# A test-time-training layer with a gated expert layer on one core: order of the expert slots and of the ending

## The reference

```python
xn = layernorm(x)
s  = attn(xn)                    # 32 heads of 8 channels, a recurrence over 16 chunks of 16 tokens
g  = silu(moe(xn))               # 8 experts, top 2, hidden width 128
out = x + s * g

# attn, per head and chunk (state W1 8x8, b1 8):
Z1      = xk @ W1 + b1
grad    = ln_fused_l2_bwd(Z1, xv - xk, ln_w, ln_b)       # needs mean and deviation of Z1
Z1_bar  = xq @ W1 - eta * tril(xq @ xk.T) @ grad + b1 - tril(eta) @ grad
W1, b1  = W1 - (eta_last * xk).T @ grad, b1 - sum(eta_last * grad)
rows    = xq + ln(Z1_bar, ln_w, ln_b)
# attn, at the end: out = ln(rows, post_w, post_b) @ o_w.T
```

## Time and profile before

| | |
|---|---|
| time, median of 3 runs | 230.91 us (230.84 to 236.54) |
| profiled execution | 232.3 us, of which span from first to last instruction 230.4 us |
| busy in the span | PE 84%, DVE 86%, ACT 48%, POOL 67% |
| granted TensorE clock, mean | 0.937 of full speed |

### The profile page before, as it was taken

How to read it: one execution, slowest core, us unless ns; L and a number is a source line. 1 busy time by engine, 2 the same in 40 slices (tenths; PEclk the granted TensorE clock), 3 DMA queues, 4 the chain that set the end, 5 groups by cost and what they waited for, 6 DMA issues and landing times.

```text
span 230.4 us, 5314 instructions
## 1 busy us (share of the span) xinstructions
PE 194.5 (84%) x1893; PEld 154.6 (67%) x1893; DVE 198.2 (86%) x542; ACT 111.7 (48%) x219; POOL 154.3 (67%) x212
## 2 busy tenths in 40 slices
PE   8734999778489989599999998999798599998772
PEld 6513666256488869577977886889586488866551
DVE  2999999999993999999999999999999999306961
ACT  2461279642428263447534976355464456147220
POOL 2314539898659749495876289879999776464234
PEclk9965999999889999889988999999999799979998
DMA  5995200226622000365030043103000300400022
GB/s 177 372 405 170 69 4 0 49 56 139 209 42 81 3 0 9 93 109 76 9 92 3 0 100 138 48 6 92 4 4 6 93 3 0 149 36 3 0 92 91
DMA packets 26001, 17.45 MB, mean 76 GB/s; under 512 B 10552, under 2 KB 24312, under 8 KB 25464
## 3 DMA queue, kind: packets, MB, share of 16 engines
q1 hardware_dynamic: 25464, 16.25, 24.9%
q10 hardware_dynamic: 512, 0.87, 1.2%
HBM read 15.22 MB, written 1.87 MB: 74 GB/s over the span
## 4 chain that ended last, share of the span: by engine, by line
DVE 63%; PE 20%; issue 8%; ACT 3%; DMA 2%; POOL 2%; DVEq 0%; POOLq 0%; SPq 0%; ACTq 0%
DVE bank L833 7%; DVE pr L885 7%; DVE dW L890 7%; DVE pr L822 6%; PE bank L1179 6%; PE bank L1220 4%; PE bank L1138 3%; PE bank L1192 3%; DMA small<-in_small 2%; DVE QP L774 2%; DVE S L849 2%; PE bank L1206 2%; PE bank L1256 2%; DVE bank L880 2%; DVE bank L876 1%
## 5 line engine op out<-in xcount | busy, mean ns | idle before, releaser
L1179 PE MATMUL bank<-xn_hi,gup_hi 128*128 128x256 f32 x128 | 41.0, 321 | 2.4 <-ACT up L583 2.4
L1192 PE MATMUL bank<-down,hT 128*128 128x256 f32 x128 | 35.4, 403 | 4.1 <-ACT G L587 3.7
L351 POOL TENSOR_TENSOR gw<-gate,share 128x256 f32<-128x256 f32 x32 | 23.3, 728 | 22.1 <-ACT gate L582 21.4
L1179 PE MATMUL bank<-xn_lo,gup_hi 128*128 128x256 f32 x128 | 36.9, 289 | 0.0
L1179 PE MATMUL bank<-xn_hi,gup_lo 128*128 128x256 f32 x128 | 36.9, 288 | 0.0
L291 POOL TENSOR_TENSOR A<-A,mask 128x256 f32<-128x256 f32 x32 | 23.3, 734 | 10.7 <-ACT A L566 10.6
L1179 PEld LDWEIGHTS bank<-xn_hi,gup_hi 128*128 128x128 f32 x128 | 25.0, 196 | 8.0 <-issue 4.9
L1192 PEld LDWEIGHTS bank<-down,hT 128*128 128x128 f32 x128 | 23.5, 202 | 6.6 <-issue 3.8
L566 ACT ACTIVATE A<-bank,one 128x256 f32<-128x256 f32 x32 | 15.1, 471 | 25.2 <-PE bank L1138 25.2
L356 POOL TENSOR_TENSOR hT<-gw,up 128x256 f32<-128x256 f32 x32 | 23.4, 730 | 4.0 <-PE bank L1192 1.7
L1179 PEld LDWEIGHTS bank<-xn_hi,gup_lo 128*128 128x128 f32 x128 | 25.2, 197 | 0.3
(11 more groups left out here) (159 smaller groups left out, 429.8 us busy)
## 6 DMA issues: line engine op xcount, KB each, us to landing
wblk<-w_blocks SPq DMA_DIRECT2D x8, 512.0 KB, 3.9
share<-shares SPq DMA_DIRECT2D x8, 512.0 KB, 8.4
sgpad<-in_gup SPq DMA_DIRECT2D x1, 1024.0 KB, 9.5
G<-in_gup SPq DMA_DIRECT2D x1, 1024.0 KB, 11.6
down<-in_down SPq DMA_DIRECT2D x1, 1024.0 KB, 14.3
xkT<-in_x_bt SPq DMA_DIRECT2D x1, 1024.0 KB, 4.9
out<-G SPq DMA_DIRECT2D x4, 256.0 KB, 2.4
wkv<-in_wkv ACTq DMA_DIRECT2D x1, 512.0 KB, 4.0
```

Of the source, the lines that this page charges most:

```text
L351: pool.tensor_tensor(gw[:, :], gate[:, i % 2, :], share[:, pair % 2, e, :], ALU.mult).then_inc(S_["gw"], 1)
L1179: ins = pe.matmul(bank[4 + i % 2][:, 2 * P * g:2 * P * g + 2 * P], w[:, k, e, NI * g:NI * g + NI].bitcast(F32R), x[:, k, 2 * pair:2 * pair ...
L1192: ins = pe.matmul(bank[7][:, HS * r:HS * r + HS], hT[:, i % 2, P * r:P * r + P], down[:, e, :], start=(e == 0 and r == 0), stop=(e == NE - ...
```

## The change

1. **ScalarE, loop**: for j = 2, 3, 5 and 6 the slot behind tile 4 (slots 6, 11, 21 and 26) goes ahead of the square root table and `step_std(2j+2)`. In j = 4 the gate of slot 14 goes ahead of `half_out(0)`.
2. **TensorE, loop**: `group_end(j-1)` goes behind tile 2 and, for j > 1, behind the second slot of the group; for j = 1 it goes behind tile 2.
3. **GpSimd**: `pad_grads(7)` goes ahead of the last `hidden_product`.
4. **Ending**: ScalarE moves rows 2 and 3 (behind `norm_z(1)`, ahead of `output_rows(3)`), not VectorE; the sums of squares go by halves of the heads, the first of them behind the first square alone; both roots wait for both sums; all eight `gate_rows` stand behind the last `post_rows`; rows 0 and 1 are projected into bank 6; three more products of zeros stand between the last transposes and the last projections; the last row's addition is VectorE's; the last two rows are written by a DMA each.

```diff
@@ sync
-            for f in range(0, NF, 2):
+            for f in range(0, NF - 2, 2):
                 sp.wait_ge(S_["fin"], f + 2)
                 sp.dma_start(out_d[:, f:f + 2, :], G[:, f:f + 2, :]).then_inc(S_["out"], 16)
-            sp.wait_ge(S_["out"], 16 * NF // 2)
+            sp.wait_ge(S_["fin"], NF - 1)
+            sp.dma_start(out_d[:, NF - 2, :], G[:, NF - 2, :]).then_inc(S_["out"], 16)
+            sp.wait_ge(S_["fin_last"], 1)
+            sp.dma_start(out_d[:, NF - 1, :], G[:, NF - 1, :]).then_inc(S_["out"], 16)
@@ gpsimd
+                if j == NG - 1:
+                    pad_grads(NG - 1)
                 for i in slots:
                     hidden_product(i)
-            pad_grads(NG - 1)
             half_scale(1)
             pool.wait_ge(S_["xt"], 16)
-            for f in range(NF):
+            for f in range(NF - 1):
                 residual(f)
@@ scalar, norm_z, post_rows and loop
-                    act.wait_ge(S_["zv"], 2 * u + k + 1)
+                    act.wait_ge(S_["zv"], 2 * u + 2)
...
-                act.wait_ge(S_["yTp"], f + 1)
+                act.wait_ge(S_["yTp"], f + 1 if f >= 4 else 4)
...
                     scores_out(j, 2)
+                    expert_slot(slots.pop(0))
                     if j == 4:
                         half_out(0)
-                    expert_slot(slots.pop(0))
                 scores_out(j, 3)
                 expert_slot(slots.pop(0))
                 if j != 4:
                     scores_out(j, 4)
+                if slots and j != 4 and j < NG - 1:
+                    expert_slot(slots.pop(0))
                 if j < NG - 1:
                     preload_sqrt(2 * j + 1)
                     step_std(2 * j + 2)
...
             norm_z(1)
+            post_rows(2)
+            post_rows(3)
             output_rows(3)
@@ vector
+                sums = zv[:, :, :].rearrange("p w (k h) -> p (w k) h", k=2)
+                squares = zsq.rearrange("p w (k h d) -> p (w k) h d", k=2, d=HD)
                 for k in range(2):
-                    v.wait_ge(S_["zc"], 4 * u + 2)
-                    v.tensor_reduce(zv[:, k, :], zsq[:, k, :].rearrange("p (a d) -> p a d", d=HD), AX.X,
+                    v.wait_ge(S_["zc"], 4 * u + k + 1)
+                    v.tensor_reduce(sums[:, :, HH * k:HH * k + HH], squares[:, :, HH * k:HH * k + HH, :], AX.X,
                                     ALU.add).then_inc(S_["zv"], 1)
...
             half_variance(1)
-            post_rows(2)
-            post_rows(3)
             second_half_rows(0)
-            gate_rows(0, 2)
             second_half_rows(1)
             half_normalise(1, 0)
             half_normalise(1, 1)
-            gate_rows(2, 4)
             post_rows(6)
             post_rows(7)
-            gate_rows(4, NF)
+            gate_rows(0, NF)
+            v.wait_ge(S_["xt"], 16)
+            v.wait_ge(S_["res"], NF)
+            v.tensor_tensor(G[:, NF - 1, :], G[:, NF - 1, :], x_tok[:, NF - 1, :], ALU.add).then_inc(S_["fin_last"], 1)
@@ tensor
-                if f < B:
-                    pe.wait_ge(S_["yTv"], 8)
-                else:
-                    pe.wait_ge(S_["yTa"], 4)
-                    pe.wait_ge(S_["yTv"], 12)
+                pe.wait_ge(S_["yTv"], 4 * (f // B) + 4)
+                pe.wait_ge(S_["yTa"], 4 * (f // B) + 4)
...
                 tile(j, 1)
-                if j == 1:
-                    expert_slot(slots.pop(0))
-                group_end(j - 1)
                 if 2 <= j < NG - 2:
                     next_pair_rows(j + 2)
-                tile(j, 2)
                 if j > 1:
+                    tile(j, 2)
                     expert_slot(slots.pop(0))
+                else:
+                    expert_slot(slots.pop(0))
+                    tile(j, 2)
+                group_end(j - 1)
                 tile(j, 3)
...
             for f in range(4, NF):
                 post_channels(f)
+            zero_products(3, 2)
             for f in range(4, NF):
                 project(f)
```

More of the change, by code:

```diff
@@ L191, in build @@
             sgT sgp z0 z zc shareTp shareTc share_d share00 share01 share10 share11 gu gact gw h y g
-            zg zv zs zr orow post0 osum ov os yn yTp yTa yTv o res fin out"""
+            zg zv zs zr orow post0 osum ov os yn yTp yTa yTv o res fin fin_last out"""
         S_ = {n: sem("s_" + n) for n in names.split()}
@@ L205, in y_rows, with o_rows @@
             return bank[f_bank(f)][:, P * k:P * k + P]
+        def o_rows(f):
+            return bank[6][:, 256 * f:256 * f + 256] if f < 2 else bank[f_bank(f)][:, 256:512]
         @block.sync
@@ L277, in _ @@
                     sp.dma_start(x_tok[:, :, :], x_bt_d).then_inc(S_["xt"], 16)
-            for f in range(0, NF, 2):
+            for f in range(0, NF - 2, 2):
                 sp.wait_ge(S_["fin"], f + 2)
                 sp.dma_start(out_d[:, f:f + 2, :], G[:, f:f + 2, :]).then_inc(S_["out"], 16)
-            sp.wait_ge(S_["out"], 16 * NF // 2)
+            sp.wait_ge(S_["fin"], NF - 1)
+            sp.dma_start(out_d[:, NF - 2, :], G[:, NF - 2, :]).then_inc(S_["out"], 16)
+            sp.wait_ge(S_["fin_last"], 1)
+            sp.dma_start(out_d[:, NF - 1, :], G[:, NF - 1, :]).then_inc(S_["out"], 16)
+            sp.wait_ge(S_["out"], 16 * (NF // 2 + 1))
         @block.gpsimd
@@ L989, in gate_rows @@
                 for f in range(first, end):
-                    v.wait_ge(S_["o"], f + 1)
+                    v.wait_ge(S_["o"], max(f + 1, 2))
                     v.wait_ge(S_["g"], f // 2 + 1)
-                    v.tensor_tensor(G[:, f, :], bank[f_bank(f)][:, 256:512], G[:, f, :], ALU.mult).then_inc(S_["res"], 1)
+                    v.tensor_tensor(G[:, f, :], o_rows(f), G[:, f, :], ALU.mult).then_inc(S_["res"], 1)
             post_count = [0]
@@ L1249, in project @@
             def project(f):
-                if f < B:
-                    pe.wait_ge(S_["yTv"], 8)
-                else:
-                    pe.wait_ge(S_["yTa"], 4)
-                    pe.wait_ge(S_["yTv"], 12)
+                pe.wait_ge(S_["yTv"], 4 * (f // B) + 4)
+                pe.wait_ge(S_["yTa"], 4 * (f // B) + 4)
                 for k in range(KC):
-                    ins = pe.matmul(bank[f_bank(f)][:, 256:512], yT[:, f // B, k, f % B].rearrange("p b t -> p (b t)"), wo[:, k, :],
+                    ins = pe.matmul(o_rows(f), yT[:, f // B, k, f % B].rearrange("p b t -> p (b t)"), wo[:, k, :],
                                     start=(k == 0), stop=(k == KC - 1))
@@ L1331, in _, with zero_products @@
                 project(f)
-            def zero_products(count):
+            def zero_products(count, bk=1):
                 for _ in range(count):
-                    pe.matmul(bank[1][:, 0:256], pe_warm[:, 0:P], pe_warm[:, :], start=True, stop=True)
+                    pe.matmul(bank[bk][:, 0:256], pe_warm[:, 0:P], pe_warm[:, :], start=True, stop=True)
             pe.wait_ge(S_["zc"], 8)
```

## The result

| | before | after |
|---|---|---|
| median of 18 runs each, same chips | 233.39 us | 228.99 us |
| profiled execution (span) | 232.3 us (230.4) | 227.8 us (225.9) |
| mean granted TensorE clock in it | 0.937 | 0.953 |

The ratio is 0.985, 95% interval 0.982 to 0.988: the change is about 3.4 us faster at 231 us. The ratio uses of each kernel only the runs within 1.5% of its fastest (9 of the changed kernel's 18) and the medians use all, so the medians lie 4.4 us apart. The prediction said 5.1 us less, 225.9 us. Its base was the median of three runs, 230.91; over 18 runs the same kernel has 233.39.

What follows compares the result with a forecast made beforehand. Bound: VectorE's recurrence, then TensorE's lag behind it and the ending's chain across engines. 4.0 us to the end of group_end(7) plus 1.1 in the ending make 5.1 off 230.9: 225.9 us, range 223.5 to 229.5.

Steps and rivals of the forecast that it cites:

- Bound, and TensorE's stop at slot 26: Groups 6 and 7: with slot 26 ahead, TensorE no longer stands until 181.34 and reaches group 7 some 4 us earlier.
- the 1.95 us for tile 3 of group 7: Group 7: tile 3 would start at 192.33 instead of 194.28, limited by step_std(15), 1.95 us earlier.
- End of `group_end(7)`: Last gradients' product: 208.57 less 1.17, 1.95, 0.45 and 0.45, so 204.6, 4.0 us earlier; itself 3.1 instead of 3.55 us.
- Stall at j = 5: Group 5: the gate ahead of the deviation makes VectorE stall 0.7 us (bounds 0 and 1.8).
- Group 1, 1.17 us: Group 1: tile 2 ahead of the gradients starts tile 3 earlier, cutting VectorE's 3.45 us stall to 2.28, gain 1.17 us.
- Padding, 0.45 us: Group 7: padded gradients fill GpSimd's idle stretch, so TensorE's 0.45 us wait for sgpad goes.
- Ending, 1.1 us: After the last gradients' product: 0.9 plus 0.2 us gained, 1.1 us (bounds −0.5 and 2.0).
- Tail: Last rows: GpSimd's seven additions end at Z + 17.7, row 6's DMA follows, row 7's is issued at Z + 18.05.
- The zeros' cost of 0.3 to 0.4: Between last transposes and last projections: three more products of zeros cost 0.3 to 0.4 us.
- From the profiled execution to the median: Whole kernel: the 5.1 us found against the 232.3 us profiled execution was taken off the median, 230.91.
- Rivals: Late deviation 228.2 (0.22); ending without gain 227.0 (0.15); more gain 224.0 (0.12); low clock in project(0..3) 235 (0.05); unchanged 230 (0.04).
- Chances: Whole kernel, 2% line at 226.3 us: faster 0.45, within 2% 0.50, slower by over 2% 0.05; forecast itself 0.42.

Runs made afterwards that it cites:

- e9_again: Changed kernel with GpSimd's second scaling product of the ending held until VectorE's first product is done, run again: ratio 0.982 to the kernel before.
- loop-only kernel: Kernel before with only the loop's edits (order of slots, gradients' product, last padded gradients), the ending as before: ratio 0.994 to the kernel before.
- e9_scale_waits: Changed kernel with GpSimd's second scaling product of the ending held until VectorE's first product is done, first run: ratio 0.977 to the kernel before.

## Why the prediction was right or wrong

- **Bound, and TensorE's stop at slot 26**: right, and by the ratios the edit on which most hangs. Undoing the gate ahead brings the stop back (3.40 us) and costs 3.1 us. The term was too large as a gain of order: the 1.95 us for tile 3 of group 7 was taken against a row whose way there had gone through slot 26 at the lower clock. With zeros in that stop the clock held and tile 3 came 1.0 us earlier against VectorE's recurrence (step 12 at 158.98 and tile 3 at 194.08, before 158.15 and 194.21).
- **End of `group_end(7)`**: predicted 204.6, measured 204.67 in the profiled execution. It is right by luck, two errors that cancel: tile 3 of group 7 came 1.1 us late, because the clock fell at 187 to 191 us (where it held, in `e9_again`, tile 3 was on time), and the product itself took 2.2 instead of 3.1 us, because the clock did not fall there.
- **Stall at j = 5**: predicted 0.7, measured 0.71 and 0.70 in the changed kernel's two profiles and 0.68 to 0.72 in the others where the clock held in group 5 and the gate stood ahead. The upper bound of 1.8 was too low: 3.81 where it fell. I had bounded it by TensorE's missing lead, not by its clock.
- **Group 1, 1.17 us**: this step failed, though the number came out (1.13 in the profile), which is luck. I counted as a gain of order that tile 3 would follow `group_end(0)` without a wait. The profile before had `group_end(0)` at the lower clock (3.38 us) and the one after had not (2.19); that is 1.2 us, less 0.3 for a later start. At equal clock the old order took 3.91 us to slot 2 and the new one 3.65 to 4.44, 3.70 and 3.80 in the changed kernel, because a pause of 0.57 to 1.36 us inside tile 3 took the place of the wait of 0.59. No wait of the program stands there; what the pause is stays open.
- **Padding, 0.45 us**: right; the wait comes back when the order is undone. The ratio has 1.5 us for it, but with an interval from nothing to over 3 us.
- **Ending, 1.1 us**: it is 0.6 in the profile (21.2 us from the end of `group_end(7)` instead of 21.8), and this step failed by mechanism. With Z the end of `group_end(7)`, I let VectorE read GpSimd's result at Z + 3.0, which it did (207.73), and kept the product's duration at the 1.07 us of the earlier trace rows, a row where GpSimd overlapped only its first half. With full overlap it was 1.68; the statistics ended at Z + 9.5 instead of 8.8. The Trainium skill states such contention ("GPSIMD Engine Reference", 1. Specifications: its SBUF interfaces are shared with VectorE, with contention for VectorE's instructions with two SBUF inputs); this product has two SBUF inputs, and the runs agree: 1.68 beside GpSimd, 0.69 when GpSimd is held. The rows of before could have priced it: the product ended 0.55 us after GpSimd's second one there too, and the end of that one in the new ending could be placed.
- **Tail**: GpSimd as last, with row 6's DMA behind it and row 7's behind that, was foreseen (Z + 18.05; measured 18.65, by the late statistics). The zeros' cost of 0.3 to 0.4 was nil (3.29 us without them and 3.30 with).
- **From the profiled execution to the median**: the largest step that failed. The sum was made against an execution 1.4 us above the median of the three runs, and the whole difference was then taken off the median. But in that execution the clock had fallen in group 1, behind slot 26 and at `group_end(7)`, the very places from which I took gains; the zeros in slot 26 took away the last two, in the profile 2.4 us. So the difference between the two profiled executions is in part chance. The profiles differ by 4.5 us, the runs by 3.4 (by the ratio). Of the missing 1.7 us, 0.6 is the ending and 1.1 this. Which fall makes up how much of the 1.1 isn't shown.
- **Rivals**: none is what happened. Projections at the lower clock did occur, but in another place and kernel (the last four, in the loop-only kernel). The Trainium skill's rule on transposes ("TensorE: Matmul & The Clock Gate", Part 4: PE-mode transpose), which I set aside since the clock had held once, may be what is behind it; one fall in four profiles neither shows nor excludes it.
- **Chances**: within 2% at 0.5 was right; the central value stood beyond the 2% that I had called even. The parts named for "faster" add up to 0.40 (0.23 + 0.12 + 0.05), not to 0.45.

The best version, by ratio over two sets of runs, is the changed kernel with GpSimd's second scaling held (0.977 and 0.982); without group 5's gate ahead it is 0.977 in one set, and with both edits and zeros 0.977 in one. All are ahead of the kernel before; against the changed kernel the trace shows the 1.0 us of the scaling and the ratios only make it likely.

## What to carry to other kernels

Before moving a step ahead of a wait on another engine, ask what the moved step hangs on: here VectorE, which had been free of TensorE, took over TensorE's clock, 0.7 us when it held and 3.8 when it fell. When an ending is packed tighter, price each instruction at its duration beside its new neighbours, from a row with full overlap, or see in a row with partial overlap by how much it outlasts its neighbour. And make a difference from one profiled execution only after asking which of its rows are chance: rows at the lower clock are not gains. A term that comes out to the hundredth can still be wrong: undo the edit and compare at equal clock.

## What the runs showed of the hardware

- The same program with the same waits gets the lower clock in one execution and not in the next. In `e9_scale_waits` and `e9_again`, one program, TensorE waited 1.30 us ahead of 185.8 and 185.6 us; the granted clock was then 0.50 from 186 to 190 us in the first and 1.00 in the second. In the kernel before, 30 executions with the same mean clock of 0.937 took from 230.05 to 232.81 us, 231.6 on the mean, and 10 with 0.930 took 231.0: the mean clock alone does not tell the time.
- VectorE's 128x512 product of two SBUF tiles takes 0.69 us alone and 1.67 to 1.70 us beside GpSimd's 128x512 product, when that one started first; GpSimd's stays at 1.25 to 1.27 us (two in 2.50 to 2.54). In seven profiles with 0.5 to 1.1 us of overlap VectorE's ended 0.54 to 0.56 us after GpSimd's. When GpSimd's began 0.13 us after a product of VectorE (`e9_again`), VectorE's took 0.69 and GpSimd's 1.71.
- The time to landing of the output's DMAs was 2.2 us for 128 KB and 2.5 us for 256 KB in the changed kernel.
